# Per-image convolution on TensorE: x0 in five pieces, and all four weight shares of the first part summed by diagonals in PSUM

## The reference, cut to what matters

```python
B, CIN, COUT, H, W, K, KH, KW = 32, 64, 64, 56, 56, 4, 3, 3
v = _gn(x)                       # 32 groups of 2 channels: (x - mean) / sqrt(var + eps)
pooled = v.mean(axis=(2, 3))
a = relu(pooled @ fc1_w.T + fc1_b)
att = softmax(a @ fc2_w.T + fc2_b)              # (B, 4)
agg_w = einsum('bk,koihw->boihw', att, weight)  # a 3x3 kernel of its own for every image
agg_b = att @ bias
out = x + conv3x3(v, agg_w, padding=1) + agg_b
```

## Time and profile before

| | |
|---|---|
| time, median of 3 runs | 305.23 us (304.73, 305.23, 305.49) |
| the profiled execution | 304.7 us, span 302.9 us |
| granted clock of TensorE, mean | 0.998 |
| TensorE busy | 297.3 us (98%) |
| VectorE, ScalarE, GpSimd busy | 246.0, 189.8, 17.7 us |
| chain that ended last | 95% TensorE, line 1063 alone 94% |

### The profile page before, as it was taken

One profiled execution on the slowest core, in us unless ns is written; L12 is line 12 of the kernel. 1 busy time (PEld: TensorE's weight loads), 2 busy tenths in 40 slices (PEclk: granted clock), 3 DMA queues, 4 the chain that ended last, 5 costly groups with the idle time before them and its releaser, 6 DMA issues.

```text
span 302.9 us, 15877 instructions
## 1 busy us (share of the span) xinstructions
PE 297.3 (98%) x7066; PEld 273.2 (90%) x7066; DVE 246.0 (81%) x799; ACT 189.8 (63%) x246; POOL 17.7 (6%) x30
## 2 busy tenths in 40 slices
PE   8899999999999999999999999999999999999995
PEld 6678997799978997799999999999999999999874
DVE  3898998989999999998998989699696978956000
ACT  3766739194683927385496869567685866768222
POOL 2221040402100000000000000000000000000000
PEclk9999999999999999999999999999999999999999
DMA  7957875737547575846808898685758342332333
GB/s 266 307 166 191 284 231 161 218 131 197 161 150 224 161 208 173 225 157 170 239 26 236 243 232 276 155 257 164 209 135 235 96 122 70 111 101 80 95 112 104
DMA packets 26868, 53.62 MB, mean 177 GB/s; under 512 B 6064, under 2 KB 16432, under 8 KB 26800
## 3 DMA queue, kind: packets, MB, share of 16 engines
q1 hardware_dynamic: 26576, 52.53, 58.6%
q10 hardware_dynamic: 224, 0.07, 0.1%
HBM read 26.89 MB, written 25.69 MB: 174 GB/s over the span
## 4 chain that ended last, share of the span: by engine, by line
PE 95%; DMA 2%; DVE 1%; SPq 0%; issue 0%; POOL 0%; ACT 0%; DVEq 0%
PE acc L1063 94%; DMA x<-x 2%; SPq L315 0%; DVE stats L443 0%; PE tiny L1004 0%; PE acc L1031 0%; PE acc L1043 0%; POOL rstd L414 0%; DVE mv L478 0%; DVE o L791 0%; ACT wh L863 0%; PE tiny L1016 0%; DVE mix L642 0%; PE tiny L1010 0%; DVE sums L490 0%
## 5 line engine op out<-in xcount | busy, mean ns | idle before, releaser
L1063 PE MATMUL acc<-xh,wh 64*64 64x385 f16 (+5 forms) x2304 | 112.6, 325 | 0.3 <-ACT wh L863 0.3
L1063 PE MATMUL acc<-xh,wl 64*64 64x385 f16 (+5 forms) x2304 | 112.4, 325 | 0.0
L1063 PE MATMUL acc<-xl,wh 64*64 64x385 f16 (+5 forms) x2304 | 111.7, 325 | 0.0
L1063 PEld LDWEIGHTS acc<-xl,wh 64*64 64x64 f16 x2304 | 91.4, 107 | 5.9
L1063 PEld LDWEIGHTS acc<-xh,wl 64*64 64x64 f16 x2304 | 90.6, 107 | 6.7
L1063 PEld LDWEIGHTS acc<-xh,wh 64*64 64x64 f16 x2304 | 89.6, 107 | 7.4 <-ACT wh L863 0.5
L913 ACT ACTIVATE o<-acc,par 128x392 f32<-128x392 f32 (+1 forms) x64 | 43.0, 672 | 56.8 <-PE acc L1063 56.8
L457 DVE BATCH_NORM_STATS2 stats<-x 128x6 f32<-128x448 f32 x105 | 61.2, 618 | 1.9
L834 ACT ACTIVATE xh<-x,xof,xsc 128x1568 f16<-128x1568 f32 x24 | 40.5, 1692 | 25.2 <-DVE xof L544 24.7
L701 DVE TENSOR_TENSOR xl<-x,xh 128x1568 f16<-128x1568 f32 x28 | 49.8, 1783 | 3.4 <-ACT x L801 3.2
L592 DVE SCALAR_TENSOR_TENSOR mix<-w_sb,ex,mix 128x576 f32<-128x576 f32 (+1 forms) x69 | 42.9, 621 | 0.5
(11 more groups left out here) (106 smaller groups left out, 161.8 us busy)
## 6 DMA issues: line engine op xcount, KB each, us to landing
x<-x SPq DMA_DIRECT2D x60, 392.0 KB, 4.1
out<-o SPq DMA_DIRECT2D x36, 196.0 KB, 3.8
out<-o SPq DMA_DIRECT2D x72, 98.0 KB, 2.8
out<-o SPq DMA_DIRECT2D x8, 588.0 KB, 3.7
out<-o SPq DMA_DIRECT2D x16, 294.0 KB, 4.3
x<-x SPq DMA_DIRECT2D x3, 448.0 KB, 4.5
w_sb<-w_t SPq DMA_DIRECT2D x2, 576.0 KB, 3.9
out<-o SPq DMA_DIRECT2D x7, 112.0 KB, 2.2
```

What stands on the lines that cost most here:

```text
L1063: ins = nc.tensor.matmul(pixels[:, top:bottom, left:right], weights[i][halves[m], tap * C:(tap + 1) * C], window, start=start and step == ...
```

## The change

x0 comes in five pieces of 2, 2, 1, 1 and 1 chunks. TensorE multiplies the diagonals of all four shares with the weights, and the sum goes to columns 64 to 255 of `tiny[0]`. It stays there: ScalarE makes the first part of `wh`, and VectorE that of `wl`, from PSUM (`mixed_part`). `part_mix` and VectorE's three operations on it are gone. `exsum` is taken before the diagonals. `first_range` takes the deviation first and the weights' bound last; the bound by itself (WEIGHTS) is now `weights_range`, written to `tiny[0]` behind the first three groups of wl*xh. The warming products are 38, 4, 6, 2, 4 and not 38, 8, 12, 6, 3, 3.

```diff
--- before.py
+++ after.py
@@ -29,8 +29,8 @@
-PIECES = ((0, 2), (2, 4), (4, 5), (5, 7))
-PIECE_OF = (0, 0, 1, 1, 2, 3, 3)
+PIECES = ((0, 2), (2, 4), (4, 5), (5, 6), (6, 7))
+PIECE_OF = (0, 0, 1, 1, 2, 3, 4)
@@ -46,16 +46,15 @@
-SUMMED_SHARES = 2
 SMALL = FC2 + K * (K + 1)
...
 SUMS = K + 2
-PART_SUM = slice(0, 3 * C)
+PART_SUM = slice(64, 64 + 3 * C)
...
 X_RING = 4
-WARM_PRODUCTS = (38, 8, 12, 6, 3, 3)
+WARM_PRODUCTS = (38, 4, 6, 2, 4)
@@ -98,7 +97,7 @@
-    return n * K - min(n, 1) - max(0, n - 2) if p == 0 else K * (mixtures(p - 1) + n) - 2
+    return K * max(0, n - 1) - max(0, n - 2) if p == 0 else K * (mixtures(p - 1) + n) - 5
@@ -135,9 +134,8 @@
-        diagonals = sb("diagonals", [P, SUMMED_SHARES, C])
+        diagonals = sb("diagonals", [P, K, C])
         eye_exsum = sb("eye_exsum", [P, C])
-        part_mix = sb("part_mix", [P, 3 * C])
         wh = [sb(f"wh{i}", [P, TAPS * C], fp16) for i in range(2)]
...
@@ -267,6 +266,10 @@
+        def mixed_part(p, n):
+
+            return tiny[0][:, PART_SUM] if (p, n) == (0, 0) else mix[:, PARTS[n]]
+
         def upper_rows(p, g, groups=1):
@@ -575,7 +578,7 @@
                     nc.vector.reciprocal(rsum[:], exsum[:]).then_inc(dch, 1)
-                    dve.wait_ge(s_range, 3)
+                    dve.wait_ge(s_range, 1)
                     nc.vector.reciprocal(rtotal[:], total).then_inc(dch, 1)
@@ -624,22 +627,15 @@
                 dve.wait_ge(s_exp, 1)
-                part = PARTS[0]
                 dve.wait_ge(s_const, 3)
-
-                for k in range(SUMMED_SHARES):
+                nc.vector.tensor_reduce(exsum[:], ex[:], AX.X, ALU.add).then_inc(s_exsum, 1)
+
+                for k in range(K):
                     nc.vector.tensor_scalar(diagonals[:, k, :], eye[:], ex[:, k:k + 1], None, ALU.mult).then_inc(s_diagonal, 1)
-                nc.vector.tensor_reduce(exsum[:], ex[:], AX.X, ALU.add).then_inc(s_exsum, 1)
+                for k in range(2):
+                    first_scale_step(k)
+                dve.wait_ge(s_weights[0], 16)
                 dve.wait_ge(s_weights[1], 16)
-                nc.vector.tensor_scalar(part_mix[:], w_sb[:, 2, part], ex[:, 2:3], None, ALU.mult).then_inc(s_part, 1)
-                first_scale_step(0)
-                dve.wait_ge(s_part, 1)
-                nc.vector.scalar_tensor_tensor(out=part_mix[:], in0=w_sb[:, 3, part], scalar=ex[:, 3:4], in1=part_mix[:],
-                                               op0=ALU.mult, op1=ALU.add).then_inc(s_part, 1)
-                first_scale_step(1)
-                dve.wait_ge(s_part, 2)
-                dve.wait_ge(s_part_sum, 2)
-                nc.vector.tensor_tensor(mix[:, part], acc[SLOTS - 1][1][:, PART_SUM], part_mix[:], ALU.add).then_inc(s_part, 1)
                 for n, part in enumerate(PARTS[1:], 1):
@@ -675,13 +671,13 @@
                 part = PARTS[n]
-                nc.vector.scalar_tensor_tensor(out=wl[0][:, part], in0=mix[:, part], scalar=wsc[0][:], in1=wh[0][:, part],
+                nc.vector.scalar_tensor_tensor(out=wl[0][:, part], in0=mixed_part(0, n), scalar=wsc[0][:], in1=wh[0][:, part],
                                                op0=ALU.mult, op1=ALU.subtract).then_inc(s_wl, 1)
...
-                dve.wait_ge(s_range, 3)
-                nc.vector.tensor_scalar(wbound[:], tiny[1][:, WEIGHTS:WEIGHTS + 1], 1.0 / C, None,
+                dve.wait_ge(s_weights_range, 1)
+                nc.vector.tensor_scalar(wbound[:], tiny[0][:, WEIGHTS:WEIGHTS + 1], 1.0 / C, None,
                                         ALU.mult).then_inc(s_bound, 1)
@@ -851,7 +847,7 @@
                     if p == 0:
-                        act.wait_ge(s_part, shares(0, 1))
+                        act.wait_ge(s_part_sum, 2)
                     else:
@@ -860,7 +856,7 @@
                 part = PARTS[n]
-                nc.scalar.activation(wh[i][:, part], mix[:, part], ACT.Copy, scale=wsc[i][:]).then_inc(s_wh, 1)
+                nc.scalar.activation(wh[i][:, part], mixed_part(p, n), ACT.Copy, scale=wsc[i][:]).then_inc(s_wh, 1)
@@ -1012,29 +1008,33 @@
-                pe.wait_ge(s_wnorms, 1)
-                nc.tensor.matmul(tiny[1][:, WEIGHTS:WEIGHTS + 1], scale[:], wnorms[:],
-                                 start=True, stop=True).then_inc(s_range, 1)
-                nc.tensor.matmul(tiny[1][:, RANGE:RANGE + 1], scale[:], wnorms[:], start=True, stop=False)
+
                 pe.wait_ge(s_first_std, 1)
...
                     nc.tensor.matmul(tiny[1][halves[m], RANGE:RANGE + 1], ones[halves[m], 0:C], std[0][halves[m], :],
-                                     start=False, stop=True).then_inc(s_range, 1)
+                                     start=True, stop=False)
+                pe.wait_ge(s_wnorms, 1)
+                nc.tensor.matmul(tiny[1][:, RANGE:RANGE + 1], scale[:], wnorms[:], start=False, stop=True).then_inc(s_range, 1)
+
+            def weights_range():
+
+                nc.tensor.matmul(tiny[0][:, WEIGHTS:WEIGHTS + 1], scale[:], wnorms[:],
+                                 start=True, stop=True).then_inc(s_weights_range, 1)
...
                 part = PARTS[0]
-                pe.wait_ge(s_weights[0], 16)
-                for k in range(SUMMED_SHARES):
+                for k in range(K):
+                    pe.wait_ge(s_weights[k // 2], 16)
                     pe.wait_ge(s_diagonal, k + 1)
                     for m in range(2):
-                        nc.tensor.matmul(acc[SLOTS - 1][1][halves[m], PART_SUM], diagonals[halves[m], k, :], w_sb[halves[m], k, part],
+                        nc.tensor.matmul(tiny[0][halves[m], PART_SUM], diagonals[halves[m], k, :], w_sb[halves[m], k, part],
                                          start=k == 0, stop=False)
...
                 for m in range(2):
-                    nc.tensor.matmul(acc[SLOTS - 1][1][halves[m], centre], eye_exsum[halves[m], :], eye_std[halves[m], :],
+                    nc.tensor.matmul(tiny[0][halves[m], centre], eye_exsum[halves[m], :], eye_std[halves[m], :],
                                      start=False, stop=True).then_inc(s_part_sum, 1)
@@ -1097,9 +1097,6 @@
             keep_warm(4)
-
-            pe.wait_ge(s_part, 2)
-            keep_warm(5)
@@ -1120,6 +1117,8 @@
                     products(0, g, wl, xh, steps)
+                if n == 0:
+                    weights_range()
```

More of the change, by code:

```diff
@@ L215, in dynamic_conv @@
         s_exsum = sem("s_exsum")
+        s_weights_range = sem("s_weights_range")
         s_eye_exsum = sem("s_eye_exsum")
```

## The result

The changed kernel took 306.44 us (median of 20 runs, 304.82 to 308.23), the kernel before 305.03 (20 runs, 304.73 to 306.00): ratio 1.0036, 95% interval 1.0021 to 1.0050. It is slower, by 1.4 us between the medians (1.1 us by the ratio). I had forecast 305.1 and no change, with a range up to 306.0.

A forecast was written before the change was run, and what follows sets the result against it. The prediction took a stream of TensorE matmuls, entered at 14.26 us, to bound the kernel. Its terms, -0.60 + 0.70 - 0.39 + 0.30, summed to +0.01 us, so it forecast 305.1 us, no change, range 304.4 to 306.0.

The forecast's parts named there:

- x0 pieces: Loading x0 in five pieces lets the last bn_stats pair end at 8.03 and not 8.47: -0.44 us.
- To the exponentials: From statistics to exponentials: steps move by 0.44 us, exponentials from 11.39 to 10.95, with ScalarE's later squares hidden by 0.1.
- Start of the sum: TensorE's diagonal sum starts at about 11.62 and not 12.22, with fewer warming products ahead: -0.60 us, containing the -0.44.
- Four shares: TensorE sums four shares and not two, at 0.35 us a share: +0.70 us, give or take 0.04.
- VectorE's sum goes: Before wh, VectorE's addition of the other two shares leaves the chain: -0.39 us.
- the PSUM source: ScalarE reads PSUM and not SBUF for wh: no difference, bounds -0.05 and +0.05 us.
- The matmul in the stream: Product with scale for the weights' bound, moved from the head to behind the first wl: +0.30 us, bounds 0.06 and 0.38.
- Rival 3: Added matmul hides for all but 0.06 us, first product comes 0.38 earlier: -0.3 us, 304.8 us; chance 0.18.
- Sum: Whole kernel: -0.60 + 0.70 - 0.39 = -0.29, and +0.30 gives +0.01 us; bounds -0.32 and +0.48.
- Rival 1: TensorE's clock falls in the head before the first product: slower, 306.5 to 307.2 us; chance one in ten.

The follow-up runs named there:

- the front of the head filled: Five versions of the changed kernel with more warming products ahead of the sums; ratios to the kernel before 1.0010, 1.0006, 1.0015, 0.9988 and 0.9998.
- the back filled: Changed kernel with the warming products ahead of the diagonal sum raised from 2 to 6: 306.06 us, ratio 1.0032 to the kernel before.
- unfilled: The changed kernel unedited, with its warming products 38, 4, 6, 2, 4: 306.44 us in the first 20 runs, 306.20 us in 12 more.
- the old kernel thinned: Kernel before with only its warming products cut, from 38, 8, 12, 6, 3, 3 to 38, 4, 6, 2, 3, 1: 306.08 us, ratio 1.0033.

## Why the prediction was wrong, by its own steps

- **x0 pieces**, -0.44: bn_stats ended at 8.01 instead of 8.47, -0.46. Right, with some luck: 0.06 of it is the first piece's earlier landing, so the split is worth 0.40 in these two traces.
- **To the exponentials**: hidden squares, 10.93 for 10.95. Right.
- **Start of the sum**, -0.60: -0.49. The diagonals were ready as expected (11.34), but TensorE began 0.14 us after the first was done (11.59 to 11.73 in the chain of waits), which I had taken as 0.02.
- **Four shares**, +0.70: four took 1.32 us (11.73 to 13.05), two had taken 0.70: +0.62. Near, but outside the 0.04 that I had allowed.
- **VectorE's sum goes**, -0.39, and the PSUM source, 0 within 0.05: from the start of the eye_exsum product to the start of wh it was 0.83 us (12.92 to 13.75) and is 0.36 (13.05 to 13.41), -0.47. Besides the addition, the wait of the reader behind TensorE got shorter: 0.12 us for VectorE before (13.24 to 13.36), 0.05 for ScalarE now (13.36 to 13.41). wh takes 0.42 and not 0.46. Together the first product moved by -0.38, where I had -0.29.
- **The matmul in the stream**, +0.30 with a bound of 0.38: 15.40 to 17.30 is 1.90 us where 15.78 to 17.27 was 1.49, so +0.41. Mis-sized, and outside my upper bound: two weight loads of 192 ns are not all that it holds up. Rival 3 had the first product right (0.38 earlier) and this matmul wrong (0.06).
- **Sum**, +0.01: -0.38 + 0.41 = +0.03, and the end of the stream moved from 299.56 to 299.61 (268.55 + 31.06). The undisturbed sum came out right by luck as much as by its terms: the head gained 0.09 us more than forecast, and the matmul in the stream cost 0.11 more.
- **Rival 1, the clock, chance 0.1**: this is where the prediction failed. The sum has no term for TensorE's clock, and the clock fell in 12 of the first 20 executions and in 19 of 32 in all. Since that is more than half, the median of the 20 is a disturbed execution, 1.4 us above that of before. The step in the text was "0.41 us idle with a microsecond of small fp32 work behind it left the clock up". It reads one execution of a kernel with twice the warming behind the statistics as evidence on another with half of it, and takes a clock that held once for one that always holds. I had counted the products (70 to 54) and measured the gap to come (1.1 us, measured 0.9 to 1.0), and then gave both little weight. The price, 306.5 to 307.2, was near for the middle step (306.3 to 306.7), and the step at 308.2 lay above it. I had read the 0.24 us from product to product at the start as the 1.2 GHz level, though the granted clock is shown as 1.00 there (2 to 3 us, before). The disturbed trace bears the reading out: at a granted clock of 0.50 the four products from 13.83 to 14.79 take 0.24 us each.

The Trainium skill, TensorE: Matmul & The Clock Gate, section "A second HAM failure mode: psum-queue depth-cycling", describes a kernel whose frequent short idles between groups of matmuls made the clock drop and come back. This case's traces agree in direction: 0.50 from 12 to 13 us on, up again within 16 to 17, behind the idles of 1.03 and 0.39 us. I had cited it for the rival and given the rival 0.1.

## What to carry to other kernels

Work that exists only to keep TensorE's clock up is on the critical path by what it prevents, and its removal must be priced as that. A single profile can't price it, because the same program keeps its clock in one execution and loses it in the next: look at many executions' mean clocks. Too many such products queue ahead of the real work: with 60 ahead of the sums these began 0.38 us after they were ready (9.80 to 10.18), with 54, tied in small groups to the events that the engine waits for, 0.05 us after (10.06 to 10.11). But x0 landed 0.26 us later in the second of these executions, so what the small groups by themselves are worth isn't shown. And a one-column fp32 matmul on 128x128 weights cost 0.41 us inside the dense stream, by two pairs of traces; moved to the head it left the median 0.5 us lower.

## What the runs showed of the hardware that I had not expected

- The same program's executions fall into steps of about 1.5 to 1.7 us, with mean clocks of 1.0, 0.994 and 0.989.
- With the front of the head filled, 0 of 55 executions lost the clock (five kernels of 11), with the back filled 6 of 12, unfilled 19 of 32, the old kernel thinned 5 of 5, and the old kernel as it was 1 of 64. In both traces of a fall the clock came down between 12 and 14 us, when TensorE was busy again (with the diagonal sum and the products behind it), and not in the sparse stretch before.
- Executions with the clock at 0.998 or more still differ by 1 us (304.74 to 305.73 in the kernel before), and two traces lose 0.27 and 0.37 us inside the dense stream, between 179 and 216 us.
- Reading 192 columns from PSUM took ScalarE 0.42 us, from SBUF 0.46.
- The landing of the last x0 piece varied by 0.4 us between two executions with the same pieces (7.29 and 7.67), which is nearly as large as the terms of this change (0.41 to 0.62).
